# A convolution block's attention loop rewritten: fp32 t and P instead of fp16 pairs, stacked halves behind a transfer, u beside the next step's scores

## The reference, cut to what matters

```python
def _L0_conv_ref(z, ln_w, ln_b, Wq, Wk, Wv, Wg, bg, Wo, bo):      # z (16, 32, 32, 32), H = 8, C = 16
    zn = (z - mu) * jax.lax.rsqrt(var + EPS) * ln_w + ln_b
    q, k, v = zn @ Wq, zn @ Wk, zn @ Wv
    g = sigmoid(zn @ Wg + bg)
    att = jnp.einsum('iabhc,jabhc->ijabh', q, k) * (1.0 / np.sqrt(C))
    att = jax.nn.softmax(att, axis=1)
    o = jnp.einsum('ijabh,jabhc->iabhc', att, v) * g
    return o.reshape(n, l, l, H * C) @ Wo + bo

x = x + _L0_conv_ref(_gn(x), ...)
x = x + _L1_conv_ref(_gn(x), ...)
return x
```

## Time and profile before

| | us |
|---|---|
| median of 3 runs (345.01 to 345.47) | 345.29 |
| the profiled execution | 347.44 |
| its span, first to last instruction | 345.5 |

### The profile page before, as it was taken

The page is one execution under the profiler, slowest core; times in us unless marked ns, Lnnn a source line. Parts: engine busy times, 40 slices in busy tenths (PEclk is TensorE's granted clock), DMA queues, the critical chain, the costliest instruction groups (busy, mean ns, idle before and its releaser), DMA issues.

```text
span 345.5 us, 7455 instructions
## 1 busy us (share of the span) xinstructions
PE 249.6 (72%) x2982; PEld 151.5 (44%) x2982; DVE 258.1 (75%) x466; ACT 217.3 (63%) x392; POOL 195.8 (57%) x169
## 2 busy tenths in 40 slices
PE   0056965599779779679679669769864599998724
PEld 0046342377347346346346347346531145554223
DVE  4985789766797898898898895899796764431972
ACT  4635787389569669669579669468341447567512
POOL 6890564659885896886877843434840862000620
PEclk9995799658998999999999998998997599999856
DMA  7100122013031031031031022100000014667207
GB/s 248 31 0 30 33 63 63 0 39 86 0 93 32 2 92 35 1 93 32 5 88 34 30 64 55 40 0 3 2 2 0 1 30 93 169 183 199 62 0 243
DMA packets 34893, 19.66 MB, mean 57 GB/s; under 512 B 21228, under 2 KB 31788, under 8 KB 34860
## 3 DMA queue, kind: packets, MB, share of 16 engines
q1 hardware_dynamic: 34860, 19.20, 20.7%
HBM read 8.71 MB, written 6.29 MB: 43 GB/s over the span
## 4 chain that ended last, share of the span: by engine, by line
DVE 41%; PE 36%; ACT 14%; issue 7%; DMA 1%; POOL 1%; DVEq 0%; ACTq 0%
PE PS L1126 31%; DVE t_sb L876 6%; DVE nmax L892 5%; DVE S_sb L896 4%; DVE og L869 4%; DVE gn_part L964 3%; DVE sums L820 3%; ACT u_sb L593 2%; ACT PP L623 2%; DVE Z L1113 2%; DVE Z L1117 2%; PE PS L1390 2%; ACT t_sb L607 2%; PE PS L1195 1%; DVE st L830 1%
## 5 line engine op out<-in xcount | busy, mean ns | idle before, releaser
L1126 PE MATMUL PS<-znT,A_bd 128*128 128x512 f16 x192 | 46.9, 387 | 11.8 <-DVE t_sb L876 10.5
L427 POOL TENSOR_TENSOR S_sb<-S_sb,rden 128x512 f32<-128x512 f32 x32 | 35.5, 1133 | 27.7 <-DVE rden L838 27.7
L876 DVE TENSOR_TENSOR t_sb<-PS,t_sb 128x512 f16<-128x512 f32 x64 | 41.1, 683 | 8.6 <-ACT t_sb L607 8.6
L607 ACT CAST t_sb<-PS 128x512 f16<-128x512 f32 x64 | 36.6, 611 | 15.0 <-PE PS L1126 13.5
L613 ACT ACTIVATE S_sb<-S_sb 128x512 f32<-128x512 f32 x32 | 20.2, 631 | 31.8 <-DVE S_sb L896 31.8
L1126 PE MATMUL PS<-zbd,t_sb 128*128 128x64 f16 x768 | 28.9, 199 | 13.6 <-DVE t_sb L876 12.8
L433 POOL TENSOR_TENSOR PP<-S_sb,PP 128x512 f16<-128x512 f32 x28 | 31.8, 1158 | 12.0 <-ACT PP L601 12.0
L1126 PEld LDWEIGHTS PS<-zbd,t_sb 128*128 128x128 f16 x768 | 26.0, 102 | 25.1 <-DVE t_sb L876 16.7
L1126 PE MATMUL PS<-PP,Z 128*128 128x128 f16 x512 | 34.6, 236 | 0.2 <-DVE PP L850 0.2
L593 ACT COPY u_sb<-PS 128x512 f32<-128x512 f32 x64 | 33.7, 626 | 1.6 <-PE PS L1126 1.4
L1126 PEld LDWEIGHTS PS<-znT,A_bd 128*128 128x128 f16 x192 | 16.9, 99 | 40.6 <-DVE t_sb L876 23.9
(11 more groups left out here) (198 smaller groups left out, 529.5 us busy)
## 6 DMA issues: line engine op xcount, KB each, us to landing
Z<-zn_dram SPq DMA_DIRECT2D x64, 64.0 KB, 2.8
x_tok<-in_x SPq DMA_DIRECT2D x4, 512.0 KB, 5.6
zn_dram<-zn_tok SPq DMA_DIRECT2D x8, 256.0 KB, 2.0
zbd<-znT SPq DMA_DIRECT2D x32, 64.0 KB, 2.0
k_dram<-og SPq DMA_DIRECT2D x4, 512.0 KB, 3.6
th<-k_dram SPq DMA_DIRECT2D x16, 128.0 KB, 2.7
out_x<-u_sb SPq DMA_DIRECT2D x4, 512.0 KB, 3.3
PP<-u_sb SPq DMA_DIRECT2D x8, 128.0 KB, 2.4
```

The source lines that it names most:

```text
L427: nc.gpsimd.tensor_tensor(P, P, bcast(rden[:, 32 * k:32 * k + 32], 2, N), ALU.mult).then_inc(p_nrm, 1)
L607: nc.scalar.copy(t_sb[:, HI, :, h], bank_tg(h)[:, :].rearrange("p (q i) -> p q i", i=N)).then_inc(t_hi, 1)
L876: nc.vector.tensor_tensor(t_sb[:, LO, :, h], bank_tg(h)[:, :].rearrange("p (q i) -> p q i", i=N), t_sb[:, HI, :, h], ALU.subtract).then_in ...
L1126: return nc.tensor.matmul(o, l, r, start=start, stop=stop)
```

## The change

**Storage.** `t_sb` and P (`S_sb`) stay fp32, so t, scores, PT and u are plain fp32 products: the casts L601, L607's low half L876, and the low half of P are gone. `S_sb` is doubled. ACT copies t (8 copies of 128x512 a period). PT is 16 fp32 transposes of pairs of positions; u is 32 fp32 matmuls whose two 64-row halves use different rows of the array and different banks. Of the eight copies of u, ACT makes five and DVE three.

**Stacked halves.** The tokens are still split into fp16 halves for t and the gates, but after the transpose: ACT writes the high half `zhl` and an fp32 copy `zTf`, DVE the low half. Then twelve transfers of 32x512 fp16 stack HI, LO and HI on 96 partitions (`zst`), for each of four e. Against weights stacked as HI, HI, LO one matmul with 96 rows does what three did: t is four 32-column tiles per head, a gate one 128x512 matmul.

**Order.** u of step j-1 now runs in period j, between the scores of step j; o and out of step j-2 come between the t's. The tokens of step j+1 are transposed as the last work of period j. The layer norm is ordered anew (the centring moves from DVE to POOL), and the statistics are added up in `acc` by POOL, with two reductions at the end instead of two a period. The loops are unrolled; the last of ten periods has only o and out.

The diff, cut to the transfers, the handling of the transposed tokens, and PE's functions:

```diff
...
-        def sp_store(sp, j, par):
-
-            wait_zn(sp, j)
-            sp.dma_start(zn_dram.rearrange("n f s k e m -> (n f) s (k e m)")[:, bass.ds(j, 1)],
-                         zn_tok[:, par].rearrange("p k e d b -> p (k e d b)").unsqueeze(1)).then_inc(zn_st[par], 16)
-
-        def sp_period(sp, j, par, half, last=False):
-
-            sp.wait_ge(zT_ok, j + 1)
-            if j == 1:
-                sp.wait_ge(s_mm, 4)
+        def sp_feed(sp, j):
+
+            par, half = j % 2, j // 2
+            wait_z(sp, j)
+            for r in range(2):
+                sp.dma_start(zn_dram[j, r].rearrange("n f b e d -> (n f) (b e d)"),
+                             zc[r::2, par].rearrange("p b e d -> p (b e d)")).then_inc(zn_st[par], 16)
+            sp.wait_ge(zT_l, j + 1)
+            for p, k in enumerate((HI, LO, HI)):
+                for e in range(A2):
+                    sp.dma_start(zst[D * p:D * p + D, par, e], zhl[D * e:D * e + D, k]).then_inc(zs_ld[par], 16)
+            if j >= 1:
+                sp.wait_ge(s_mm, 4 * j)
             for e in range(A2):
                 rows = slice(D * e, D * e + D)
-                sp.dma_start(zbd[rows, e], znT[rows]).then_inc(zbd_ld, 16)
-            if not last:
-                sp_store(sp, j + 1, 1 - par)
-            else:
+                sp.dma_start(zbd[rows, e], zTf[rows]).then_inc(zbd_ld, 16)
+            if j >= 2:
                 sp.wait_ge(u_mm, 8 * (j - 1))
-            sp.wait_ge(zn_st[par], 16 * (half + 1))
-            for copy in range(2):
+            sp.wait_ge(zn_st[par], 32 * (half + 1))
+            for r in range(2):
                 for e in range(A2):
-                    r0 = 64 * copy + N * e
-                    sp.dma_start(Z[r0:r0 + N, par, :, :, e].rearrange("p f k d b -> p f k (d b)"),
-                                 zn_dram[:, :, bass.ds(j, 1), :, e].rearrange("n f s k m -> n (f s) k m")
+                    r0 = 64 * r + N * e
+                    sp.dma_start(Z[r0:r0 + N, par, :, D * e:D * e + D],
+                                 zn_dram[j, r, :, :, :, e].rearrange("n f b d -> n (f b) d")
                                  ).then_inc(Z_ld[par], 16)
...
+        def act_zT(act, j):
             act.wait_ge(zT_mm, j + 1)
-            src = bank_w[:, :].bitcast(f16).rearrange("p (k n f) -> p k f n", f=A4, n=N)
-            dst = znT[:, :, :].rearrange("p k c -> p (k c)").rearrange("p (k f n) -> p k f n", f=A4, n=N)
-            nc.scalar.copy(dst, src).then_inc(zT_ok, 1)
+            if j >= 1:
+                act.wait_ge(zs_ld[(j - 1) % 2], 192 * ((j - 1) // 2 + 1))
+            nc.scalar.copy(z_cols(zhl[:, HI]), zT_bank()).then_inc(zT_h, 1)
+            if j >= 1:
+                act.wait_ge(zbd_ld, 64 * j)
+            nc.scalar.copy(z_cols(zTf[:, :]), zT_bank()).then_inc(zT_f, 1)
...
+        def act_period(act, j):
+            m = j - 1
+
+            def t_copies(hs):
                 for h in hs:
                     act.wait_ge(t_mm, H * j + h + 1)
-                    nc.scalar.copy(t_sb[:, HI, :, h], bank_tg(h)[:, :].rearrange("p (q i) -> p q i", i=N)).then_inc(t_hi, 1)
-
-            def exps(ks):
-                for k in ks:
-                    act.wait_ge(s_sub, 4 * j + k + 1)
...
+        def dve_zT_low(dve, j):
+            dve.wait_ge(zT_f, j + 1)
+            nc.vector.tensor_tensor(z_cols(zhl[:, LO]), zT_bank(), z_cols(zhl[:, HI]), ALU.subtract).then_inc(zT_l, 1)
...
-        def pe_znT(pe, j, par):
-            wait_zn(pe, j)
-            if j >= 3:
-                pe.wait_ge(x1_ok, j - 2)
-            zt = bank_w[:, :].bitcast(f16)
-            tok = zn_tok[:, par].rearrange("p k e d b -> p k (e d) b")
-            for k in (HI, LO):
-                for b in range(SB):
-                    at = 128 * (SB * k + b)
-                    last = nc.tensor.transpose(zt[:, at:at + 128], tok[:, k, :, b], ident16[:, :])
+        def pe_zT(pe, j):
+            wait_z(pe, j)
+            if j >= 1:
+                pe.wait_ge(g_th, HP * j)
+            for b in range(SB):
+                last = nc.tensor.transpose(bank_w[:, 128 * b:128 * b + 128],
+                                           zc[:, j % 2, b].rearrange("p e d -> p (e d)"), ident[:, :])
             last.then_inc(zT_mm, 1)
 
-        def pe_t(pe, j, hs=range(H)):
-            if hs[0] == 0:
-                pe.wait_ge(zT_ok, j + 1)
+        def pe_t(pe, j, hs):
             for h in hs:
+                if h == 0:
+                    pe.wait_ge(zs_ld[j % 2], 192 * (j // 2 + 1))
+                if h < 3 and j >= 1:
+                    pe.wait_ge(g_th, HP * (j - 1) + 3)
+                if h in (1, 2) and j >= 2:
+                    pe.wait_ge(u_ok, 5 * (j - 1))
                 if h >= 3:
-                    pe.wait_ge(t_lo, H * j + h - 2)
-                elif j >= 1:
-                    pe.wait_ge(g_th, HP * (j - 1) + h + 2)
-                split_mm(bank_tg(h)[:, :], [A_bd[:, k, h].rearrange("p e d -> p (e d)") for k in (HI, LO)],
-                         [znT[:, k] for k in (HI, LO)]).then_inc(t_mm, 1)
+                    pe.wait_ge(t_ok, H * j + h - 2)
+                for e in range(A2):
+                    last = mm(bank_tg(h)[D * e:D * e + D, :], A_st[0:96, h], zst[0:96, j % 2, e])
+                last.then_inc(t_mm, 1)
 
         def pe_gate(pe, j, ks):
             for k in ks:
-                if k < 3:
-                    pe.wait_ge(t_lo, H * j + H - 2 + k)
-                else:
-                    pe.wait_ge(g_th, HP * j + 1)
-            for n, (w, z) in enumerate(((HI, HI), (LO, HI), (HI, LO))):
-                for k in ks:
-                    rows = slice(D * k, D * k + D)
-                    last = mm(bank_tg(H + k)[:, :], Wg_s[rows, w], znT[rows, z], n == 0, n == 2)
-                    if n == 2:
-                        last.then_inc(g_mm, 1)
+                if k == 1 and j >= 2:
+                    pe.wait_ge(x1_ok, j - 1)
+                if k == 1 and j < 2:
+                    pe.wait_ge(zT_l, j + 1)
+                if k >= 2:
+                    pe.wait_ge(g_th, HP * j + k - 1)
+                mm(bank_g(k)[:, :], Wg_st[0:96], zst[0:96, j % 2, k]).then_inc(g_mm, 1)
 
         def pe_scores(pe, j, ks):
-            if ks[0] == 0:
-                pe.wait_ge(t_lo, H * (j + 1))
-                pe.wait_ge(zbd_ld, 64 * (j + 1))
-                if j >= 2:
-                    pe.wait_ge(o_ok, HP * (j - 2) + 2)
             for k in ks:
+                if k == 0:
+                    pe.wait_ge(t_ok, H * (j + 1))
+                    pe.wait_ge(zbd_ld, 64 * (j + 1))
                 if k >= 2:
                     pe.wait_ge(s_sub, 4 * j + k - 1)
                 elif j >= 1:
-                    pe.wait_ge(s_sub, 4 * (j - 1) + k + 3)
+                    pe.wait_ge(s_sub, 4 * j)
                 for q in range(8 * k, 8 * k + 8):
-                    last = split_mm(bank_s(k)[:, 64 * (q % 8):64 * (q % 8) + 64],
-                                    [t_sb[:, p, q].rearrange("p h i -> p (h i)") for p in (HI, LO)],
-                                    [zbd[:, :, p, N * q:N * q + N] for p in (HI, LO)])
+                    last = mm(bank_s(k)[:, 64 * (q % 8):64 * (q % 8) + 64],
+                              t_sb[:, q].rearrange("p h i -> p (h i)"), zbd[:, :, N * q:N * q + N])
                 last.then_inc(s_mm, 1)
 
-        def pe_PT(pe, s, ks):
-            if ks[0] == 0 and s >= 1:
-                pe.wait_ge(o_ok, HP * s)
+        def pe_PT(pe, m, ks):
             for k in ks:
-                pe.wait_ge(p_lo, 4 * s + k + 1)
+                pe.wait_ge(p_nrm, 4 * m + k + 1)
                 if k >= 2:
-                    pe.wait_ge(pt_ok[k % 2], 2 * s + 1)
-                for q in range(8 * k, 8 * k + 8):
-                    last = nc.tensor.transpose(bank_b(k)[:, :].bitcast(f16)[:, 128 * (q % 8):128 * (q % 8) + 128],
-                                               P2[:, q].rearrange("p k m -> p (k m)"), ident16[:, :])
+                    pe.wait_ge(pt_ok, 4 * m + k - 1)
+                for i in range(4):
+                    q = 8 * k + 2 * i
+                    last = nc.tensor.transpose(bank_b(k)[:, 128 * i:128 * i + 128],
+                                               S_sb[:, m % 2, q:q + 2].rearrange("p q a n -> p (q a n)"), ident[:, :])
                 last.then_inc(pt_mm, 1)
 
-        def pe_u(pe, s, par, half):
-            pe.wait_ge(Z_ld[par], 128 * (half + 1))
-            for k in range(8):
-                if k in (0, 3):
-                    pe.wait_ge(pt_ok[k % 2], 2 * (s + 1))
-                elif k >= 4:
-                    pe.wait_ge(u_ok, 8 * s + k - 3)
-                for q in range(4 * k, 4 * k + 4):
-                    b, f = divmod(q, A4)
-                    o = bank_u(k)[:, 128 * (q % 4):128 * (q % 4) + 128]
-
-                    Zq = Z[:, par, f].rearrange("p k e d b -> p k (e d) b")[:, :, :, b]
-                    mm(o, Zq[:, HI], PT[:, q], True, False)
```

(42 more changed lines are left out.)

601 lines of the change are left out of this document (276 added, 325 removed).

## The result

| kernel | median us | runs | against before |
|---|---|---|---|
| before | 345.15 | 345.0 to 345.47 | |
| after | 423.15 | 421.64 to 424.1 | 1.2254, 95% interval 1.2215 to 1.2293 |

The account below looks back on a forecast made before the run. The prediction took DVE's work and the two-engine handling of t to bound the kernel before. Its terms were 42 + 34 + 43 + 240 + 36 + 24 + 84 = 503 us, stated as 500, range 405 to 550.

Parts of the forecast that it names:

- What DVE loses: DVE, each period: subtractions, PT copies, reductions and a centring go, copies come; net 6.6 us less, busy time down about 50.
- that DVE bounds before: Kernel before: DVE's work, nearly full at 22.1 of 25 us, and two-engine handling of t set the 25.27 us period.
- The trip: Between token transposes and next t: copies 2.3 us plus twelve transfers 8.8, so 11.1 us exposed in each of eight steps.
- PE's own parts: PE at the high clock: front 7.4 us, the rest 17.8, including scores 7.2, PT 1.8, u 5.4.
- The high period: Steady period with PE at the high clock throughout: 7.4 + 17.8 + 11.1 = 36.3 us.
- The clock: PE behind each gap: starts at 1.2 GHz, rises during PT or u; period taken as 48 us, between 36.3 and 53.6.
- The first rival: PE behind the gap: clock recovers at once as o fills the array behind the first t's; 414 us, chance 0.25.
- Rival 3: Transfers issue in half the time, about 27 us off, or u's halves queue, adding 28; no separate chance given.
- Rival 5: PE's t: column tiles don't run side by side, 6.9 instead of 1.7 us, 24 in all; no separate chance given.
- Rival 4: Whole kernel not slower: DVE's 6.6 us come off and the round trip is covered; about 342 us, chance 0.04.
- "Hidden" layer norm: Statistics on POOL, about 1.1 us per added operation: layer norm ends before the token transposes some 30 us later.
- the weights' preparation in period 0: DVE prepares the triangle weights, some 12 us, beside the first round trip; otherwise the second step's sums come 3 us late.

Follow-up runs that it names:

- no_trip_ln: Kernel after, with t and gates of every step reading step 0's stacked tokens and ACT's layer-norm square behind all eight t copies: 347.65 us (1.004 against before).
- filled: Kernel after, plus unused identity products on PE ahead of each t group (8 first, 22 later): 466.45 us (1.3494 against before).
- o_first: Kernel after, with the o products moved ahead of the first t products, into PE's wait for the transfers: 429.72 us (1.241 against before).
- o_last: Kernel after, with the o products moved behind all eight t products instead of the first three: 441.56 us (1.2738 against before).
- ahead_f16: Kernel after, with earlier token transposes, reordered transfers and square, first-step filler, fp16 scores without low bits, and layer norm begun earlier: 338.40 us (0.977 against before).
- two_queues: Kernel after, with six of the twelve token transfers issued from ACT's queue instead of SP's: 401.43 us (1.1574 against before).
- tuned: Kernel after, with token transposes behind PT's first two groups, gates in one bank, square between t copies, six first-step filler products: 356.27 us (1.0292 against before).

## Why the prediction was right in sign and wrong in size

1. **What DVE loses: right; that DVE bounds before: not tested.** DVE's busy time fell by 50.8 us (about 50 forecast), its share to 49%. No run took work off DVE in the kernel before; with the trip gone too, no_trip_ln's period is 24.5 us against 25.27.
2. **The trip: right, to 0.1 us.** 11.07 in seven places, 6.8 before the first t. Its parts were 2.2 for ACT and DVE (2.3 forecast), 0.63 an issue (0.615), 1.84 for the landing (2.0). no_trip_ln shows that it and what follows it are the loss: 75.5 of 78 us.
3. **PE's own parts: right at the high level.** The scores' pass is 0.118 (0.113 forecast), low 0.222 (0.226); u's halves run side by side, 32 passes in 2.06, so 4.4 and not 5.4; the front is 8.3 to 9.2 with a low o in it (7.4 to 10.8) and 6.6 at the high level; the rest 15.9 (17.8). The high period was put at 36.3; it was 35.7 with 2.1 us of low clock in it, so 33.6 without.
4. **The clock: this step failed.** The forecast took 48 us a period on the ground that "what follows is the same kind of work" as behind the gap in the earlier trace rows. It is not: there it was scores and gates, here it is t, then o. The low level lasted 4 or 6 us and cost 1.7 or 2.6 (filled), not 12. Of the 82 us between the sum (503) and the span (421), five steady periods are 240 - 178.5 = 61.5, period 7 is 36 - 25.5 = 10.5, and period 1, 43 against 37, another 6. That the range held the result is owed to the rival below, whose case it took in.
5. **The first rival came nearest and had 0.25.** "o fills the array right behind the first t's" was its reason; o_first and o_last, which move o and nothing else, bear it out in part. The clock did not recover at once, but after 4 or 6 us, and in two periods of o_last o did not bring it back. Its 414 lacks period 0, which has no o and took 33.5 us as forecast for the low level (26 high), and 4 us of period 1. What spoke against it (t paced by ACT, scores at loads half their time) does hold where o is missing: periods 0 and 1, and o_first. The program's order, shown with the change, was evidence for it; no row of the trace before has o behind such a gap.
6. **The Trainium skill's passage on oscillation** ("TensorE: Matmul & The Clock Gate") agreed in kind: each steady period starts at 0.50 behind its transfer wait. The Trainium skill's load, on the same page under "LDWEIGHTS (loading the stationary operand)", an estimate of 107 ns for 128 columns, is not what is seen: a pass takes 0.222 us low and 0.118 high.
7. **Rival 3** fell: the issues of smaller transfers are 0.63 apart, and the halves don't queue. **Rival 5** fell: 12 column tiles of t take 0.83. **Rival 4** (trip covered, 342) was tried by leaving the trip out: 347.65 with the square moved as well.
8. **"Hidden" layer norm: true only beside the trip.** It ended in time in the kernel after. With the trip gone its square became the next wait (385 instead of 348), and it bounds ahead_f16. The text named it as hidden but not what hid it. The same holds of the weights' preparation in period 0, which the text did name as resting on the first round trip: with it the last t's of period 1 waited 0.8 us in the kernel after, 4.3 in two_queues, 9.0 in tuned.

## What to carry to other kernels

Price a moved step by its whole chain to the consumer and count its transfers one by one: here the issues ahead of the last of twelve small ones were 6.9 of 11 us. When a wait is taken away, look at what it had been hiding on other engines' rows, since here that was worth as much as half the wait. And when PE must wait, what stands behind the wait can matter beyond its own time: moving o's 2.4 us of work into the gap made the kernel slower.
